# New keys of four heads weighed in row tiles of the TensorE array, with one bank per head for the output and one score buffer

## The reference, cut to what matters

```
q, k, v = projections of x3            # 128 query rows per key head: 4 query heads x 32 tokens
k_all = concat(k_cache[pages], k)      # 16 pages x 32 = 512 old keys, then 32 new ones
v_all = concat(v_cache[pages], v)      # 8 key heads of 128 channels
scores = q k_all^T, old keys masked past cache_seqlens[b]
o = softmax(scores) v_all              # per batch and key head: [128 queries x 544 keys] . [544 x 128]
out = x3 + o Wo^T
```

## Time and profile before

| | us |
|---|---|
| median of 3 runs | 2527.35 (2525.82 to 2528.05) |
| the profiled execution, time | 2534.27 |
| the profiled execution, span of its trace | 2532.5 |
| attention, first to last new-key matmul | 1281 |
| one group of four heads in attention, where nothing disturbs it | 10.00 |

### The profile page before, as it was taken

The page is one execution under the profiler, slowest core; times in us unless marked ns, Lnnn a source line. Parts: engine busy times, 40 slices in busy tenths (PEclk is TensorE's granted clock), DMA queues, the critical chain, the costliest instruction groups (busy, mean ns, idle before and its releaser), DMA issues. The chain is left out here.

```text
span 2532.5 us, 52304 instructions
## 1 busy us (share of the span) xinstructions
PE 2423.1 (96%) x14785; PEld 2023.1 (80%) x14785; DVE 1545.5 (61%) x3027; ACT 1161.6 (46%) x2251; POOL 1124.4 (44%) x1364
## 2 busy tenths in 40 slices
PE   5989999999999599999999999999999999899999
PEld 4337777777776498999998999999989998788887
DVE  4656299888888466666666666666666665332221
ACT  6663387778777233433433344344333433321111
POOL 0323144444444466666666666666656665000000
PEclk9999999999999799999999999999999999999999
DMA  9334233333332788888888888888888885843442
GB/s 307 100 102 170 82 104 104 93 100 98 95 94 86 229 275 270 273 274 275 271 272 269 276 274 275 274 273 276 278 254 274 275 272 179 241 126 107 133 126 65
DMA packets 475258, 501.44 MB, mean 198 GB/s; under 512 B 104373, under 2 KB 399285, under 8 KB 471094
## 3 DMA queue, kind: packets, MB, share of 16 engines
q1 hardware_dynamic: 438326, 366.38, 47.2%
q0 software_dynamic: 36864, 134.23, 16.1%
HBM read 404.02 MB, written 96.47 MB: 198 GB/s over the span
## 5 line engine op out<-in xcount | busy, mean ns | idle before, releaser
L1214 ACT ACTIVATE att_probs<-att_probs,att_low 128x544 f32<-128x544 f32 x512 | 383.2, 748 | 800.9 <-DVE att_low L1273 798.6
L1124 POOL TENSOR_TENSOR att_probs<-att_probs,att_inverse 128x512 f32<-128x512 f32 x512 | 534.4, 1044 | 392.1 <-DVE att_inverse L1287 388.7
L1273 DVE CUSTOM_DVE_ANT_0 att_probs<-att_score,att_mask,att_batch_cols 128x544 f32<-128x544 f32 x512 | 401.5, 784 | 340.7 <-PE att_score L1147 336.7
L1147 PE MATMUL att_score<-att_keys_raw,att_queries_raw 128*128 128x288 f32 (+1 forms) x2048 | 556.5, 395 | 29.9 <-DMA att_queries_raw<-q_t 29.9
L1179 PE MATMUL att_o<-att_probs_t,att_values 128*128 128x128 f32 x4096 | 541.0, 275 | 0.0
L1179 PEld LDWEIGHTS att_o<-att_probs_t,att_values 128*128 128x128 f32 x4096 | 497.6, 192 | 0.1
L1147 PEld LDWEIGHTS att_score<-att_keys_raw,att_queries_raw 128*128 128x128 f32 x2048 | 351.8, 192 | 85.4 <-DMA att_queries_raw<-q_t 31.0
L1283 DVE COPY att_probs_t<-att_turn 128x512 f32<-128x512 f32 x512 | 351.2, 686 | 1.3 <-PE att_turn L1157 1.3
L1157 PE MATMUL att_turn<-ident,att_probs 128*128 128x128 f32 x2048 | 307.8, 273 | 1.6 <-POOL att_probs L1124 1.5
L1157 PEld LDWEIGHTS att_turn<-ident,att_probs 128*128 128x128 f32 x2048 | 256.1, 141 | 54.5 <-POOL att_probs L1124 3.4
L1110 POOL DMA_INDIRECT att_values<-L_cond_v_cache,att_v_rows_of x256 | 251.5, 982 | 81.6 <-POOL att_v_rows_of L1106 49.7
(11 more groups left out here) (130 smaller groups left out, 3204.7 us busy)
## 6 DMA issues: line engine op xcount, KB each, us to landing
att_keys_raw<-L_cond_k_cache SPq DMA_DIRECT2D x1024, 128.0 KB
q_t<-proj_q_out SPq DMA_DIRECT2D x32, 1024.0 KB, 3.9
att_queries_raw<-q_t SPq DMA_DIRECT2D x64, 512.0 KB
o_t<-att_heads_out SPq DMA_DIRECT2D x64, 512.0 KB, 5.3
out_o_raw<-o_t SPq DMA_DIRECT2D x32, 1024.0 KB, 5.8
prep_natural<-L_cond_weight SPq DMA_DIRECT2D x16, 1024.0 KB, 8.6
w_nat<-L_cond_Wq SPq DMA_DIRECT2D x8, 1024.0 KB, 5.9
v_new<-values_v_out SPq DMA_DIRECT2D x16, 512.0 KB, 2.6
```

The source lines that it names most:

```text
L1124: nc.gpsimd.tensor_tensor(probs[:, k, 0:L], probs[:, k, 0:L], inverse[:, k:k + 1].to_broadcast([P, L]), ALU.mult).then_inc(probs_ready, 1)
L1147: last = nc.tensor.matmul(score_ps[n % 2][:, cols], queries_raw[j][:, h, :], keys_raw[j][:, pages, h, :], start=True, stop=True)
L1214: nc.scalar.activation(probs[:, k, :], probs[:, k, :], ACT.Exp, bias=low[k][:, 0:1], scale=-1.0, accum_out=total[k][:, 0:1]).then_inc(exp_ ...
L1273: nc.vector.tensor_tensor_reduce(out=probs[:, k, :], in0=score_ps[n % 2][:, LEFT:LEFT + KEYS], in1=mask[j][:], scale=batch_cols[j][:, h:h ...
```

## The change

It does four things in `stage_attention`. The new-key matmul of each head takes only that head's 32 rows of `new_values` and `new_probs_t`, at partitions 0, 32, 64 and 96, which makes four row tiles of the array; `new_values` shrinks to the real blocks, and the zeroing goes. Each head of a group gets an output bank of its own (512 columns apart), so that the four banks exist once and no longer twice; `weigh` of a group's first head waits until `keep_o` has copied the group before, and `keep_o` moves from `n % 4 == 3` to `n % 4 == 2`. Scores have one buffer (two banks) and the transposes one bank, the new-key transpose one of its own. Semaphores that were pairs become single ones.

```
-        new_values = [a_.sb(f"new_values{v}", [P, HK, D]) for v in range(2)]
+        new_values = [a_.sb(f"new_values{v}", [P, HK // GH, D]) for v in range(2)]
-        score_ps = [a_.ps(f"score{n}", 1024) for n in range(2)]
-        turn_ps = [a_.ps(f"turn{n}") for n in range(2)]
-        o_ps = [a_.ps(f"o{n}") for n in range(2)]
+        score_ps = a_.ps("score", 2 * BANK)
+        turn_ps = a_.ps("turn")
+        new_ps = a_.ps("new")
+        o_ps = a_.ps("o", GH * BANK)
...
-            for v in range(2):
-                nc.gpsimd.memset(new_values[v][:], 0.0).then_inc(zeroed, 1)
...
             def scores(i, n):
-                pe.wait_ge(scores_masked[n % 2], i * (N // 2) + n // 2)
+                pe.wait_ge(scores_masked, i * N + n)
...
             def turn(i, n):
-                pe.wait_ge(kept[job % 2], (i if n >= 0 else i - 1) * (JOBS // 2) + job // 2)
+                pe.wait_ge(kept, i * N + n)
...
             def weigh(i, n):
                 if h % GH == 0:
-                    pe.wait_ge(o_ready[g % 2], back * 2 + g // 2)
+                    pe.wait_ge(o_ready, back * (N // GH) + g)
+                o = o_ps[:, (h % GH) * BANK:(h % GH) * BANK + P]
...
-                    for r in range(GH):
-                        last = nc.tensor.matmul(o[:, r * P:(r + 1) * P], new_values[j][:, h - GH + 1 + r, :], new_probs_t[g % 2][:],
-                                                start=False, stop=(r == GH - 1), skip_group_check=True)
-                    last.then_inc(o_done[g % 2], 1)
+                    for r in range(GH):
+                        rows = slice(r * S, (r + 1) * S)
+                        nc.tensor.matmul(o_ps[:, r * BANK:r * BANK + P], new_values[j][rows, h // GH, :], new_probs_t[g % 2][rows, :],
+                                         start=False, stop=True, skip_group_check=True).then_inc(o_done, 1)
...
             def keep_o(i, n):
+                act.wait_ge(o_done, back * N + (g + 1) * GH)
                 if g % 2 == 0:
                     act.wait_ge(o_stored[j], back * 16)
-                nc.scalar.activation(heads_out[j][:, (g % 2) * GH:(g % 2 + 1) * GH].rearrange("d h n -> d (h n)"), o_ps[g % 2][:],
-                                     ACT.Copy).then_inc(o_ready[g % 2], 1)
+                nc.scalar.activation(heads_out[j][:, (g % 2) * GH:(g % 2 + 1) * GH],
+                                     o_ps.rearrange("d (h k) -> d h k", h=GH)[:, :, 0:P], ACT.Copy).then_inc(o_ready, 1)
             def pair(i, first):
-                    if n % GH == 3 and (n >= GH or not first):
-                        keep_o(i, n - 4)
+                    if n % GH == 2 and (n >= GH or not first):
+                        keep_o(i, n - 3)
```

More of the change, by code:

```diff
@@ L989, in stage_attention @@
     NLD = 16 * GH
-    JOBS = N + N // GH
+    BANK = 512
     with ExitStack() as ctx:
@@ L1024, in stage_attention @@
         mask_ready = a_.sem("mask_ready")
-        scores_done = a_.sem("scores_done", 2)
-        scores_masked = a_.sem("scores_masked", 2)
+        scores_done = a_.sem("scores_done")
+        scores_masked = a_.sem("scores_masked")
         exp_done = a_.sem("exp_done")
@@ L1029, in stage_attention @@
         probs_ready = a_.sem("probs_ready")
-        turned = a_.sem("turned", 2)
-        kept = a_.sem("kept", 2)
+        turned = a_.sem("turned")
+        kept = a_.sem("kept")
+        new_turned = a_.sem("new_turned")
+        new_kept = a_.sem("new_kept")
         group_ready = a_.sem("group_ready")
         weighed = a_.sem("weighed", 2)
-        o_done = a_.sem("o_done", 2)
-        o_ready = a_.sem("o_ready", 2)
+        o_done = a_.sem("o_done")
+        o_ready = a_.sem("o_ready")
         o_stored = a_.sem("o_stored", 2)
         block = ctx.enter_context(nc.Block())
-        def job_of(n):
-            return (n // GH) * (GH + 1) + n % GH
         @block.sync
@@ L1107, in load @@
                     pool.lower_val(b + 1)
-                    pool.wait_ge(zeroed, 2)
+                    pool.wait_ge(iota_done, 1)
                     pool.wait_ge(index_ready, b + 1)
@@ L1174, in weigh @@
                 if h % GH == 0:
-                    pe.wait_ge(o_ready[g % 2], back * 2 + g // 2)
-                job = job_of(m)
-                pe.wait_ge(kept[job % 2], back * (JOBS // 2) + (job // 2 + 1))
+                    pe.wait_ge(o_ready, back * (N // GH) + g)
+                pe.wait_ge(kept, i * N + (n + 1))
+                o = o_ps[:, (h % GH) * BANK:(h % GH) * BANK + P]
                 for t in range(PPT):
-                    last = nc.tensor.matmul(o[:, cols], values[j][:, t, h * D:(h + 1) * D], probs_t[m % 2][:, t * P:(t + 1) * P],
-                                            start=(h % GH == 0 and t == 0), stop=False, skip_group_check=True)
+                    last = nc.tensor.matmul(o, values[j][:, t, h * D:(h + 1) * D], probs_t[m % 2][:, t * P:(t + 1) * P],
+                                            start=(t == 0), stop=False, skip_group_check=True)
                 last.then_inc(weighed[m % 2], 1)
                 if h % GH == GH - 1:
-                    job += 1
                     if h == GH - 1:
                         pe.wait_ge(new_loaded[j], back * NLD + NLD)
-                    pe.wait_ge(kept[job % 2], back * (JOBS // 2) + (job // 2 + 1))
+                    pe.wait_ge(new_kept, back * (N // GH) + (g + 1))
                     for r in range(GH):
-                        last = nc.tensor.matmul(o[:, r * P:(r + 1) * P], new_values[j][:, h - GH + 1 + r, :], new_probs_t[g % 2][:],
-                                                start=False, stop=(r == GH - 1), skip_group_check=True)
-                    last.then_inc(o_done[g % 2], 1)
+                        rows = slice(r * S, (r + 1) * S)
+                        nc.tensor.matmul(o_ps[:, r * BANK:r * BANK + P], new_values[j][rows, h // GH, :], new_probs_t[g % 2][rows, :],
+                                         start=False, stop=True, skip_group_check=True).then_inc(o_done, 1)
             def pair(i, first):
@@ L1215, in softmax, with new_part @@
                                      accum_out=total[k][:, 0:1]).then_inc(exp_done, 1)
-            def new_part(i, n):
+            def new_part(i, n, first=False):
                 m = n % N
@@ L1221, in new_part @@
                 g = m // GH
[L1222 to L1225, removed]
+                act.wait_ge(new_turned, back * (N // GH) + (g + 1))
+                if g or not first:
+                    act.wait_ge(o_done, back * N + (g - 1) * GH)
+                nc.scalar.activation(new_probs_t[g % 2][:], new_ps[:, 0:P], ACT.Copy).then_inc(new_kept, 1)
             def keep_o(i, n):
@@ L1241, in pair @@
                     if n % GH == 1 and (n >= GH or not first):
-                        new_part(i, n - 2)
-                    if n % GH == 3 and (n >= GH or not first):
-                        keep_o(i, n - 4)
+                        new_part(i, n - 2, first)
+                    if n % GH == 2 and (n >= GH or not first):
+                        keep_o(i, n - 3)
             pair(0, True)
@@ L1266, in mask_scores @@
                 if n % GH == 0 and (n >= RING or not first):
-                    back, job = divmod(job_of((n - GH - 1) % N) + 1, JOBS) if n >= RING else (-1, job_of((n - GH - 1) % N) + 1)
-                    dve.wait_ge(turned[job % 2], (i + back) * (JOBS // 2) + (job // 2 + 1))
-                dve.lower_val(i * (N // 2) + (n // 2 + 1))
+                    dve.wait_ge(new_turned, i * (N // GH) + (n // GH - 1))
+                dve.lower_val(i * N + (n + 1))
                 dve.wait_ge(setup, 3)
-                dve.wait_ge(scores_done[n % 2], i * (N // 2) + (n // 2 + 1))
-                nc.vector.tensor_tensor_reduce(out=probs[:, k, :], in0=score_ps[n % 2][:, LEFT:LEFT + KEYS], in1=mask[j][:],
+                dve.wait_ge(scores_done, i * N + (n + 1))
+                nc.vector.tensor_tensor_reduce(out=probs[:, k, :], in0=score_ps[:, LEFT:LEFT + KEYS], in1=mask[j][:],
                                                scale=batch_cols[j][:, h:h + 1], scalar=3e38, op0=ALU.add, op1=ALU.min,
-                                               accum_out=low[k][:, 0:1]).then_inc(scores_masked[n % 2], 1)
+                                               accum_out=low[k][:, 0:1]).then_inc(scores_masked, 1)
             def main_part(i, n):
```

40 lines of the change are left out of this document (16 added, 24 removed).

## The result

The changed kernel takes 2538.35 us (2535.94 to 2540.66, 5 runs) against 2527.35 us (2525.82 to 2529.05, 5 runs): a ratio of 1.0037, 95% interval 1.0023 to 1.0051. It is slower by 11 us; the forecast was 9 us faster. The profiled execution of after took 2535.94 us, its span is 2533.8. In what follows "before" and "after" are the two kernels, e1 to e9 the experiments.

A forecast was written before the change was run, and what follows sets the result against it. TensorE's own stream was taken to set the pace, DMA engines close behind. Terms -32 + 6 + 1 + 14 + 2 = -9 us gave 2518 us from the median 2527.35; range 2496 to 2545.

The forecast's parts named there:

- What bounds the kernel: Attention: TensorE, busy 1272 of 1281 us, sets the pace at 10.00 us a group, DMA engines (88% busy) close behind.
- The store behind it: `keep_o` at the first group of each batch also waits for an earlier output store; late stores cost +14 us.
- "+2" for new values: New values are needed 0.16 to 0.25 us earlier and already come late at about ten batches: about +2 us.
- The waits cost more than the tiles bring: Rival: landings 0.5 or 0.8 us later, or no score-buffer cover; 2522 to 2545, about 2531 us; chance 0.22.
- The new-key block: Four row tiles run side by side: 0.64 us instead of 0.89, saving 0.25 a group, -32 us over 128 groups.
- One score buffer: Scores wait for the previous head's mask: 0.18 us at a pair's first head, +6 us; pipeline filling about +1.
- 0.05 x 192 = 10 us: Price of each 0.05 us of stall at three of four heads if the score buffer's 0.07 us cover were gone.
- One turn bank, one set of output banks: Next turn's load has 0.28 us spare, `keep_o` before the next group's first `weigh` 0.5: no cost (output banks: 64 groups).

The follow-up runs named there:

- e1: Changed kernel with SyncE's queue no longer checking a batch's 16 page numbers against their bounds: 2496.40 us, ratio 0.9868.
- e9: e4 with VectorE's work for the next batch's mask (`columns`) at the fourth head of a batch, not the last: 2491.24 us, ratio 0.9818.
- e2: Kernel before, without SyncE's bounds checks of the page numbers: 2519.93 us, ratio 0.9963.
- e4: Changed kernel without the page checks and with each output store issued one batch earlier: 2493.44 us, ratio 0.9852.
- e7: e4 with the new-key matmuls over all 128 rows again and zeroed `new_values`: 2530.00 us, ratio 0.9998.
- e8: e2 with one score buffer, nothing else of the change: 2527.96 us, ratio 0.9990.
- e6: Kernel before with one more, unused load of four page numbers per batch on SyncE's queue: 2635.40 us, ratio 1.0409.
- e3: Changed kernel, page checks kept, with each output store issued one batch earlier in SyncE's order: 2543.28 us, ratio 1.0041.

## Why the prediction was wrong

By its own steps:

**What bounds the kernel: this failed.** "So TensorE's own stream sets the pace, and the DMA engines stand close behind." I asked which engine was full and which DMA engines were, and never added up the queue that issues the transfers. The 20.1 to 20.2 us of SyncE's queue (e1, e2) were level with TensorE's 20.0, so the 0.25 a group that TensorE saves could not come back as time. The page leaves register and issuing instructions out of the busy time. The two rows that could have led there I had: the starts of its transfers with the gap up to the next keys, and the waits for new values, 7.9 us, which I took for slow landings. They were the symptom of a queue that had just fallen behind: in e2 they are gone, with the same transfers and sizes and a DMA share of 0.88, where before has 0.87 over the same 1000 us.

**The store behind it: the place was right, the distance wrong.** "The store is issued 12.07 after the batch's first scores" is no fixed distance. It is the median of before, where it already ran from 11.4 to 14.0. With a queue that keeps up it is nearly fixed, 11.6 to 12.2 in e1; in after its median is 12.5, and the store comes that much later against a limit that the shorter blocks had moved earlier. ScalarE waited for 39 stores, where 15 to 25 were forecast, and TensorE's loads of `weigh` 28.8 us behind it. The +14 us of late stores was to be a remainder; with a light queue it is smaller still (e1 against e4: 3 us, inside the spread), and with the full queue it is, together with the waits for new values, what makes up the difference between 19.6 and 20.2. Likewise the "+2" for new values.

**The rival that came true in size didn't in cause.** "The waits cost more than the tiles bring" had 2522 to 2545, by landings 0.5 to 0.8 later. The measured time lies near the top of the stated range only because this rival had stretched the range upwards; that is luck. The waits do eat the tiles' gain, but e1 has a higher DMA share (0.90) and loses nothing to landings.

**The new-key block: right.** 0.64 predicted, 0.63 measured: 0.10 in, two rounds, 0.10 out and the loads. The tiles' loads run side by side: in the trace the four of a round start 7 ns apart, the second round 0.11 behind the first. Two of its signs came out otherwise: the eight loads took 0.31 and not 0.25, and from the first product to the scores' start it is 1507.77 - 1507.34 = 0.43 and not 0.55 to 0.6, because both first products are recorded about 0.1 early, together with the load that nothing hides. 128 x 0.25 = 32 was predicted and 36.6 measured (e7 to e4). The Trainium skill, page "TensorEngine Tiling (Array Packing)", Key Properties, has the drain at a change of mode, and the trace agrees (the 0.10 before the loads, where the first load of a full-array block starts together with the last product of the block ahead). The Trainium skill, page "TensorE: Matmul & The Clock Gate", Part 3, gives 3.07 times for four row tiles at 512 columns; for this block of 128 columns between full-array work the trace has 0.89 / 0.63 = 1.4.

**One score buffer: right in the sum, the fill too small.** +6 and +1 predicted, 8.0 measured (e8). The 0.18 at a pair's first head is in the trace, 28 x 0.18 = 5; the fill costs more than the 1 us I gave it. These rows show it, two of after and then one of before: in after the first scores take 2.18 us, and the second head waits for the first head's mask; in before the first three heads' scores run on without a wait.

```profile
850.68 2.18 PE L1142 MATMUL att_score<-att_keys_raw,att_queries_raw 128*128 128x288 f32 x4 [27.61 <-DMA att_queries_raw<-q_t]
...
853.91 2.18 PE L1142 MATMUL att_score<-att_keys_raw,att_queries_raw 128*128 128x288 f32 x4 [1.04 <-DVE att_low L1265]
...
850.78 4.59 PE L1147 MATMUL att_score<-att_keys_raw,att_queries_raw 128*128 128x288 f32 x12 [29.07 <-DMA att_queries_raw<-q_t]
```

The longer fill goes with a low clock. TensorE had stood still for 27.6 us in after and 29.1 in before, and its granted clock was at half (1.2 GHz). The windows from 855 to 860 us, after and then before, show in the third figure from the end that in after it still is, while in before it is full again (2.4 GHz):

```profile
855.00:860.00 5.00, 4.00 (x11) 2.40 (x9) 1.54 (x4) 0.84 (x2) 2.08 (x2) 0.50 0.82 235
...
855.00:860.00 5.00, 3.92 (x25) 2.95 (x24) 3.79 (x11) 2.23 (x5) 3.25 (x4) 1.00 0.75 234
```

The first new-key block comes at 870.19 in after and at 866.65 in before, 3.5 us later, with the first scores within 0.1 us of each other. From the first scores to that block it is 15.9 us in before and e2, and 18.9 to 20.1 in all kernels with one score buffer; by the clock records the full clock is back 3 to 6 us behind the first scores in before, e2 and e6, and 9 to 13 us in those.

The price "0.05 x 192 = 10 us", should the cover of 0.07 be gone, counts half the heads: three of four of 64 x 8 are 384, so each 0.05 would cost 19 us. It stood in no sum, and the cover held.

**One turn bank, one set of output banks: nothing predicted, 2 us at most.** e7 is 2.0 above e8, inside the spread. In its trace 30 groups are 0.05 longer, as are those of 9.78 in e4; `columns` is behind them, as e9 shows: with it moved they take 9.73.

**The sum, where the queue doesn't bind:** e4 less e2 is 2493.4 - 2519.9 = -26.5 us: tiles -36.6 (e4 less e7), the buffers +10.1 (e7 less e2). My terms for these, -32 + 6 + 1, give -25. The change does what it was costed at; the sum was made against the wrong bound.

**What stays open.** The queue accounts for the lost gain: relieve it, and the change is worth 23.5 us (e1 less e2). Of the 11 us by which after is slower than before, 3.5 are the fill. The profiled executions are only 1.7 us apart (2535.94 and 2534.27) and their batches 20.20 and 20.18, because that of before lies 7 us above its median, with its waits for new values. That most executions of before lose less to the queue than this one is likely and not shown. That the register load is longer in after (median 2.42 against 2.19) would go the same way; it is one profiled execution of each. Nor was it tried why this load takes 1.0 us in one batch and 2.9 in another.

## What to carry to other kernels

Before costing a change on the engine that looks full, add up one period of every queue, the issuing ones too: each transfer, each register load, each check, against the period of the loop. If a queue's sum is level with it, as here, what the engine saves is given back, and it shows as waits on whatever that queue issues last. A wait that moves when the order is changed (e3), while the time doesn't, has its cause behind it. A check or a transfer fewer on the full queue may be worth more than the change itself: here 16 bounds checks a batch were worth 42 us to the changed kernel and 12 to the one before.

## What the runs showed of the hardware

- A bounds check of a loaded page number costs SyncE's queue 0.26 us (0.147 and 0.018 busy, the rest between them), as 16 of them 4.1 us; a page transfer 0.52 us of queue (16 in 8.25), and one with rows split over heads 0.72 (4 in 2.87).
- The register load of a batch's 16 page numbers took 1.0 to 3.2 us (median 2.0 to 2.7 by kernel), one of four numbers right behind it 0.30 (e6).
- Four row tiles of 32 rows and 128 columns, 32-bit: eight loads over in 0.31 us, the whole block 0.63 with 0.2 of emptying and 0.2 of loads that nothing hides.
- Behind some of TensorE's longer waits inside attention its granted clock fell to half. By the trace's clock records that is 3.4 us in all in before, 6.8 in after, 27 in e3 and 75 in e6, and none between the first and the last new-key block in e1, e2 and e4, where TensorE hardly waits.
